# Layer 1 operator stored in quads of steps inside a patch

## What is computed

```
def _L1_conv_ref(x, weight, bias, op_w, op_b):
    xu = _unfold(x)                                   # (b, c, h, w, 9): the nine taps of each pixel
    n = jnp.sqrt(jnp.sum(xu * xu, axis=1))            # one norm per tap, over the channels
    op = jnp.tanh(n @ op_w.T + op_b).reshape(b, h, w, K2, K2)
    x_op = jnp.einsum('bchwj,bhwjk->bchwk', xu, op)   # each pixel's own 9x9 operator
    wr = weight.reshape(c, -1, K2).transpose(1, 0, 2)
    out = jnp.einsum('bchwk,ock->bohw', x_op + xu, wr)
    return out + bias[None, :, None, None]
...
x = x + _L1_conv_ref(_gn(x), ...)
```

## Time and profile before

| what | value |
|---|---|
| median of 3 runs | 2517.36 us (2513.78 to 2520.08) |
| the profiled execution, its own time | 2509.56 us |
| its span in the trace | 2507.8 us |
| PE busy over the span | 2162.4 us (86%) |
| DVE, ACT, POOL busy | 1213.8, 1153.5, 185.8 us |
| layer 1's blocks, first piece to last mix | from 765 to 1797 us |

### The profile page before, as it was taken

How to read it: one execution, slowest core, us unless ns; L and a number is a source line. 1 busy time by engine, 2 the same in 40 slices (tenths; PEclk the granted TensorE clock), 3 DMA queues, 4 the chain that set the end, 5 groups by cost and what they waited for, 6 DMA issues and landing times.

```text
span 2507.8 us, 85342 instructions
## 1 busy us (share of the span) xinstructions
PE 2162.4 (86%) x38916; PEld 1599.1 (64%) x38916; DVE 1213.8 (48%) x2300; ACT 1153.5 (46%) x1986; POOL 185.8 (7%) x131
## 2 busy tenths in 40 slices
PE   4778699999979999999999999999457888986754
PEld 2446244444437888988888889888355666555653
DVE  3565234444455445445445444453256776552345
ACT  0111356565655545545545545544265676741210
POOL 1000000000010000000000000000222343110000
PEclk9999899999989999999999999999677898995665
DMA  6864836767452333433333433434733555287798
GB/s 133 211 172 100 155 111 171 172 159 204 119 166 37 71 57 63 73 57 65 71 58 63 72 58 61 72 59 95 182 95 122 146 153 170 69 174 199 145 287 238
DMA packets 610284, 306.13 MB, mean 122 GB/s; under 512 B 418236, under 2 KB 586054, under 8 KB 602566
## 3 DMA queue, kind: packets, MB, share of 16 engines
q1 hardware_dynamic: 599376, 283.93, 49.1%
q10 hardware_dynamic: 10560, 16.93, 2.7%
HBM read 172.28 MB, written 128.54 MB: 120 GB/s over the span
## 4 chain that ended last, share of the span: by engine, by line
PE 76%; DVE 8%; ACT 5%; SPq 4%; issue 3%; DMA 2%; ACTq 0%; DVEq 0%
PE ps L743 20%; PE ps L680 11%; PE ps L759 10%; PE ps L718 10%; PE ps L639 9%; PE ps L687 7%; ACT arena L951 4%; PE ps L798 3%; DVE arena L1485 2%; PE ps L913 2%; DMA arena<-x_dram 1%; DVE arena L1534 1%; PE ps L880 1%; PE ps L820 1%; DVE arena L1536 1%
## 5 line engine op out<-in xcount | busy, mean ns | idle before, releaser
L743 PE MATMUL ps<-arena 62*64 62x108 f32 x11008 | 561.6, 358 | 27.2 <-DMA arena<-xcl 23.0
L1407 DVE TENSOR_TENSOR arena<-arena 128x1024 f32<-128x1024 f32 (+1 forms) x308 | 353.5, 1162 | 339.3 <-ACT arena L1025 339.2
L743 PEld LDWEIGHTS ps<-arena 62*64 62x64 f32 x11008 | 477.3, 147 | 53.5 <-DMA arena<-xcl 23.4
L1033 ACT COPY arena<-ps 128x864 f32<-128x864 f32 x258 | 226.9, 880 | 347.7 <-PE ps L759 237.0
L1025 ACT ACTIVATE arena<-ps 128x1024 f32<-128x1024 f32 (+1 forms) x308 | 295.4, 976 | 179.2 <-PE ps L718 179.0
L718 PE MATMUL ps<-arena 63*64 63x128 f32 (+1 forms) x9504 | 314.2, 271 | 13.8 <-ACT arena L1025 13.5
L951 ACT ACTIVATE arena<-arena,nmr,rstd 128x128 f32<-128x128 f32 x752 | 295.1, 512 | 33.3 <-DVE nmr L1221 33.3
L718 PEld LDWEIGHTS ps<-arena 63*64 63x64 f32 x9504 | 297.1, 138 | 18.4 <-ACT arena L1025 14.9
L680 PE MATMUL ps<-arena 128*128 128x512 f32 x640 | 288.2, 596 | 14.2 <-ACT arena L965 14.2
L759 PE MATMUL ps<-arena 64*64 64x384 f32 (+1 forms) x3168 | 260.1, 477 | 1.2 <-issue 1.2
L680 PEld LDWEIGHTS ps<-arena 128*128 128x128 f32 x640 | 120.5, 189 | 166.9 <-issue 166.9
(11 more groups left out here) (135 smaller groups left out, 1775.9 us busy)
## 6 DMA issues: line engine op xcount, KB each, us to landing
arena<-xcl SPq DMA_DIRECT2D x688, 60.0 KB, 2.6
x_dram<-arena SPq DMA_DIRECT2D x16, 2048.0 KB, 7.3
arena<-x_dram SPq DMA_DIRECT2D x16, 2048.0 KB, 15.0
arena<-l_dram SPq DMA_DIRECT2D x32, 1024.0 KB, 13.5
xcl<-arena SPq DMA_DIRECT2D x8, 3072.0 KB, 10.9
arena<-in_x SPq DMA_DIRECT2D x32, 512.0 KB, 10.1
y_dram<-arena ACTq DMA_DIRECT2D x64, 256.0 KB, 5.7
arena<-in_x SPq DMA_DIRECT2D x16, 1024.0 KB, 15.8
```

Of the source, the lines that this page charges most:

```text
L743: mm = pe.matmul(ps[T2 * j:T2 * j + T2, bank + t, STEPS * uu:STEPS * uu + STEPS], xs[T2 * t:T2 * t + C + LANES, e, j, u, :], own[T2 * t:T2 ...
L1033: nc.scalar.copy(ysb[:, :, e, u:u + UG, :].rearrange("p t u s -> p t (u s)"), ps[:, bank:bank + 2, 0:UG * STEPS]).then_inc(main_out_a, 1)
L1407: nc.vector.tensor_tensor(own, own, d, ALU.add).then_inc(op_done, 1)
```

## The change

`ops` is stored with four steps of a patch side by side (QUAD = 4): 27 groups of steps, in each all patches, in each patch four steps. The patch's 108 steps that `main_op` streams are now 27 runs of four floats (16 bytes), the runs 512 floats apart.

So that ACT can go on writing contiguous runs, `fill_op` puts the four steps of a bank into each other: matmul i writes its 128 columns at i, i + 4, i + 8 and so on. `tanh_out` then reads 512 contiguous floats of each bank and writes them contiguously, as before; only the last fill (two steps in a bank) writes pairs. `add_delta` works in place on the same 1024 floats, and its second operand is now four floats of `delta` that are repeated for each patch, where it was one float repeated 128 times. No instruction is added, removed or moved on any engine or queue, and no wait is changed. The counts of columns, the weights and the PSUM banks are the same.

```
+QUAD = 4
...
-        def op_steps(m, f):
+        def op_quads(m):
 
             n = columns_of(m) * NU
-            return ops[m % 2][:, FILL * f * n:(FILL * f + 2 * fill_steps(f)) * n]
+            return ops[m % 2][:, 0:STEPS * n].rearrange("p (g x s) -> p g x s", x=n, s=QUAD)
+
+        def own_quads(m, f):
+
+            return op_quads(m)[:, 2 * f:2 * f + -(-fill_steps(f) // 2), :, :]
...
-                            mm = pe.matmul(ps[T2 * t:T2 * t + T2, fill_bank(f) + e, P * i:P * i + n],
+                            mm = pe.matmul(ps[T2 * t:T2 * t + T2, fill_bank(f) + e, i:sub * n:sub],
                                            w_op[T2 * e:T2 * e + C + LANES + 1, FILL * f + sub * e + i, :],
                                            norms[T2 * e:T2 * e + C + LANES + 1, m % 2, t, 0:n], start=True, stop=True)
...
-                own = ops[m % 2][:, 0:STEPS * n * NU].rearrange("p (s x) -> p s x", s=STEPS)
+                own = op_quads(m)
...
-                                           own[T2 * t:T2 * t + C + LANES, :, NU * (2 * e + j) + HALF_U * (i // 8) + u], start=True, stop=True)
+                                           own[T2 * t:T2 * t + C + LANES, :, NU * (2 * e + j) + HALF_U * (i // 8) + u, :], start=True, stop=True)
...
-                raw_op = ps[:, fill_bank(f):fill_bank(f) + 2, 0:P * sub].rearrange("p a (s x) -> p a s x", x=P)[:, :, :, 0:n]
-                nc.scalar.activation(op_steps(m, f).rearrange("p (a s x) -> p a s x", a=2, s=sub), raw_op, ACT.Tanh).then_inc(fill_tanh, 1)
+                raw_op = ps[:, fill_bank(f):fill_bank(f) + 2, 0:sub * n]
+                own = own_quads(m, f)
+                if sub == QUAD:
+                    own = own.rearrange("p g x s -> p g (x s)")
+                else:
+                    own = own[:, 0].rearrange("p x (a s) -> p a x s", a=2)
+                    raw_op = raw_op.rearrange("p a (x s) -> p a x s", s=sub)
+                nc.scalar.activation(own, raw_op, ACT.Tanh).then_inc(fill_tanh, 1)
...
-                own = op_steps(m, f).rearrange("p (s x) -> p s x", s=steps)
-                d = delta[:, FILL * f:FILL * f + steps].rearrange("p (s x) -> p s x", x=1).to_broadcast([P, steps, n])
+                own = own_quads(m, f)
+                d = delta[:, FILL * f:FILL * f + steps].rearrange("p (g x s) -> p g x s", x=1, s=QUAD).to_broadcast([P, steps // QUAD, n, QUAD])
```

## The result

| | before | changed |
|---|---|---|
| median | 2518.7 us (4 runs) | 2395.8 us (2395.0 to 2398.0, 4 runs) |
| ratio, 95% interval | | 0.9509 (0.9488 to 0.9530) |
| profiled execution, its span | 2509.6, 2507.8 us | 2396.2, 2394.4 us |
| a block, mean from the first to the last mix of 384 columns | 46.9 us | 41.1 us |

The changed kernel is 4.9% faster. 123 us went where 147 were forecast; 2396 us lies inside the range of 2350 to 2520, 26 us above the forecast.

What follows compares the result with a forecast made beforehand. PE was taken as the bound, its pieces paying double per column. Of 11.2 us gained a block 7.0 remain, 21 x 7.0 = 147 us; 2509.6 - 147 = 2363 us, median 7.8 higher, 2370 us; range 2350 to 2520.

Steps and rivals of the forecast that it cites:

- Part 1: Piece matmuls on PE: runs of four floats read at full rate, 1.46 to 0.76 us a piece, 11.2 us a block.
- Part 3: Fill matmuls writing PSUM in strides: no cost, a fill stays at 0.89 us.
- the rival: Fills on PE: strided PSUM writes cost double, 1.74 us a fill, 2556 us in all; chance 0.18.
- Part 4: ACT's tanh unchanged; DVE's addition with the repeated quad between 1.22 and 1.30 us.
- the rival of a slower DVE: DVE's addition: the repeated quad brings it to 1.8 us, 43.6 us a block, 2444 us; chance 0.04.
- partly: Fills on PE: 1.05 to 1.50 us each, 40.3 to 45.6 us a block, 2374 to 2485 us; chance 0.11.
- the change does nothing: Pieces on PE: the 512-float hop costs as much as a lone float, 1.46 us stays, 2517 us; chance 0.05.
- Part 2: PE's waits in a block once pieces are quick: of 11.2 us gained 7.0 remain, 40.1 us a block.
- Pixels: Next block's piece 0 on PE: waits 0.77 us for its pixels; a landing of 3.2 us instead of 2.5 adds 0.7.
- the walk: One block followed in written order: 47.0 us with today's pieces, 39.5 with quick ones, trusted to some tenths.
- ACT's copies: Pieces 2 and 10 on PE: each waits 0.46 us for the copies of pieces 0 and 8.
- DVE's copies: PE waits 0.70 us at each of pieces 5 and 13, and 0.60 at the mix behind piece 8.

Runs made afterwards that it cites:

- pairs: Changed kernel with runs of two floats instead of four in the operator and a PSUM stride of two floats; 2415.5 us, ratio 0.9592.
- the run where nothing could hide more: Kernel before, with only the fills' PSUM writes strided by four floats and the operator still in steps; 2521.9 us, ratio 1.0002.
- without pixels: Changed kernel without layer 1's loads of pixels after the first two batches, so layer 1's result differs; 2345.3 us, ratio 0.9313.
- the quads across two lines: Changed kernel with the operator's two buffers 8 bytes further on, each run of four floats straddling two 16-byte lines; 2404.5 us, ratio 0.9537.

## Why the prediction was right, and by how much it missed

**The bound and the cause: right.** PE was the bound, the piece paid double, and the cause was the moving operand. Both halves show it, one alone each: steps with strided PSUM 1.47 us, quads with plain PSUM 0.75.

**Part 1, the piece: right.** 0.76 us forecast by a line through the two fills, 0.75 measured; mean duration 255 forecast, 257 measured. The rule of the Trainium skill (SBUF — State Buffer, Specifications (TRN2)) that two accesses to a line are enough for full bandwidth agreed with the trace of before and would have given the same sum here. It is too weak: by it pairs should run at full rate, and they take 0.98 us.

**Part 3, PSUM in strides: right, and the rival falls.** 0.89 us forecast, 0.87 measured, and 0.89 in the run where nothing could hide more. The rule in the Trainium skill (PSUM — Partial Sum Buffer, Specifications (TRN2)), that any access that isn't contiguous slows matmuls, doesn't hold for float32 writes four floats apart. The argument from the pace, 0.84 ns a column, fits, but no run varied the pace, so it stays an argument.

**Part 4: right.** Tanh 1027 and addition 1221 ns, so the rival of a slower DVE falls. The rival *partly* falls by the fill's 0.87 us, and *the change does nothing* by the piece's 0.75.

**Part 2, the waits: the mechanism was right, two terms had the wrong size and one was missing.** 4.3 us a block were counted, allowance included, and 5.7 were lost. The rows name only 4.9 of them, so the terms are compared by how late each group starts, start to start, read from the trace for every group and averaged over the 19 blocks from the second to the twentieth:

- Pixels: 1.4 counted (0.8 and the allowance of 0.6), 2.0 measured. Ahead of piece 0 it is 1.6; the last DMA of a batch lands late (3.4 us in the block shown, where the sum had 2.5 and the allowance 3.2). Piece 8 waits for its own batch too in 7 of the 19 blocks, 0.4 us on average, where the walk had none.
- ACT's copies: 0.9 counted, 1.1 measured.
- DVE's copies: 2.0 counted, 1.0 measured. Pieces 5 and 13 are late by 0.4 and 0.5 us, not by 0.70 each, and the mix by under 0.1, not by 0.60. That PE loses time elsewhere explains little of it: without pixels it is still 0.4 and 0.5, and 0.2 at the mix. Why the walk has these copies later than they are wasn't worked out.
- Issue: none counted, 1.3 measured. This is the term that the walk lacked.

The work itself came out at 35.4 us, not 35.8. That the walk gave 47.0 us with slow pieces tested none of these terms, since nothing waits there. So it is partly luck that the block is as near to the forecast as it is: the 1.0 us too much for DVE hid most of the 1.3 us that were missing for issue.

The forecast for the profiled execution was 2363 us, and it took 2396.2, 33 more. The blocks are 21 of these (41.1 us for 40.1, 21 times). Some 14 us lie outside layer 1: the first piece starts at 770.5 instead of 765.0 us, and 719 instead of 711 us follow the last mix. The same kernel run again began at 771.7 us, and others of this study between 765.5 and 773.2, so I take it for scatter of runs; it wasn't studied. The median is off by only 26 us because the forecast added 7.8 us for the distance of the median from the profiled execution, which is 0.4 us in the changed kernel; that is luck.

**What the issue gaps are.** The gaps grow as the records get shorter. In the full blocks (787 to 1595 us, 1608 and 1620 where blocks are longer) they come to 0.6 us where a piece and a fill take 64 records in 2.36 us (36.9 ns a record, the steps), to 2.6 with pairs (1.86 us, 29 ns), to 5.6 with the quads across two lines (1.71 us, 27 ns) and to 13.8 with quads (1.62 us, 25 ns). In the timeline of the changed kernel they come in pairs four microseconds apart:

```profile
1004.39 0.89 PE L723 MATMUL ps<-arena 63*64 63x128 f32 x24 [0.45 <-issue]
...
1008.51 0.48 PE L723 MATMUL ps<-arena 63*64 63x128 f32 x9 [0.65 <-issue]
```

and in the page's list of queues the instructions are fetched in packets of 4.83 MB / 295 = 16.4 KB:

```profile
q8 instruction: 295, 4.83, 0.9%
```

They are longest where records are shortest, at the last block's fills of 64 columns (piece and fill in 1.23 us, 19 ns a record):

```profile
1606.16 0.28 PE L723 MATMUL ps<-arena 63*64 63x64 f32 x3 [2.10 <-issue]
```

The trace has each of these packets, and they tell what PE waits for. Between 1000 and 1004 us there is one, in the 18th of the 40 slices, at 1001.8 us; its 1.8% of 16 engines' 4 us make 1.15 us, so it ends at 1002.9, and the gap ends at 1004.39:

```profile
DMA  0000000000000000070000000000000000000000
q8 instruction: 1, 0.02, 1.8%
```

It is so every time: all 34 issue gaps of the changed kernel between 787 and 1640 us end 1.2 to 1.6 us after the end of an instruction packet. So PE waits there for its instructions. How fast they come is an estimate. Between 787 and 1620 us there are 173 packets for 22008 matmul records, 127 a packet, so quads use one up in 127 x 25 ns = 3.2 us, quads across lines in 3.4, pairs in 3.7, steps in 4.7. Where gaps follow each other, their ends are 4.0 to 4.4 us apart, and no two packets start less than 3.4 us apart. A supply of one packet in some 4 us, with something in store from the mixes, would give the gaps as they are. Why it isn't faster stays open; a packet itself takes 1.1 us with the pixels' loads and without, though nearly half of the gaps went with them.

## What to carry to other kernels

Compare matmuls by nanoseconds per column and tile, start to start: a group that pays twice what its neighbours pay at the same clock may have its cause in how its operands lie, and here four floats side by side, aligned to 16 bytes, were enough to cure it. When the bound engine becomes twice as fast in one group, walk one period in the written order with the other engines' durations: here 11.2 us of gain became 5.8, and the order that was balanced for slow pieces wanted its fills one piece later.

## What the runs showed of the hardware

- The read of a float32 moving operand, by length of run with a hop of 512 bytes or more between: 1.69 ns a column and tile for one float, 1.13 for two (0.98 us x 4 / 32 / 108), 0.97 (0.84 us) for four across a 16-byte boundary, 0.87 for four inside one, where contiguous fills have 0.85 to 0.87. Neither "two per line" (0.87 for two) nor a fixed price of a hop on top of the full rate (1.28 for two) gives all four.
- Writing PSUM from float32 matmuls four floats apart costs nothing measurable (0.89 us a fill with and without), and neither does ACT's reading it four or 128 floats apart (1025 and 1028 ns for 1024, 1024 contiguous).
- PE can outrun its own instructions: at 25 ns a pair of matmul and weight load it idled 13.8 us in 808 us, each time until 1.2 to 1.6 us after a packet of 16.4 KB of instructions had ended; at 37 ns a pair it idled 0.6 us in 833.
- A wait costs more than its length where the clock falls behind it. In the changed kernel piece 0 at 1135.87 waited 2.62 us for pixels; in the stretch after it (columns: us, busy, granted clock, DMA share, GB/s) the clock was partly at its lower level, 1.2 GHz, and the fill and the mix took 1.62 and 7.25 us where they take 1.06 and 5.99. It is rare: over 787 to 1620 us the granted clock is 1.00, rounded.

```profile
1133.00:1137.00 4.00, 1.38 (x58) 1.00 0.50 78
1137.00:1141.00 4.00, 4.00 (x52) 0.57 0.57 89
```

```profile
1135.87 0.97 PE L748 MATMUL ps<-arena 62*64 62x108 f32 x32 [2.62 <-DMA arena<-xcl]
1136.63 1.62 PE L723 MATMUL ps<-arena 63*64 63x128 f32 x32
1137.95 7.25 PE L764 MATMUL ps<-arena 64*64 64x384 f32 x72
```
